# Summing the sampled corner values by accumulating transposes in place of f32 matmuls with the identity

## The chip, the cores and the metric

The kernel runs on one core of a Trainium2 chip. The metric is the device time of one execution in microseconds. The engines are named as in the profile: PE is TensorE (PEld its weight loads), DVE VectorE, ACT ScalarE, POOL GpSimd, SP SyncE.

## The reference

Two layers are applied to an image batch `x` of shape (2, 64, 64, 256), all in f32. The first is a deformable attention: q, k and v maps come from a projection and a depthwise 3x3 convolution; for each pixel, each of 8 groups and each of 9 sample points, k and v are read at a shifted, fractional position. The second layer is a normal attention over 4096 tokens per image with convolutions around it, and then a layer of 8 experts. The change touches only the sampling of the first layer:

```python
out = v00*(1-wx)*(1-wy) + v01*wx*(1-wy) + v10*(1-wx)*wy + v11*wx*wy   # four corners of a sample
...
attn = jnp.einsum('bgpc,bgpkc->bgpk', qh, k)
attn = jax.nn.softmax(attn, axis=-1)                                 # over the 9 samples
out = jnp.einsum('bgpk,bgpkc->bgpc', attn, v)                        # sum over the 9 samples
...
return out @ proj_w + proj_b
```

Four corners times nine samples are the 36 corners of a pixel and a group. Weight of a corner and softmax weight are multiplied first, so the output of a pixel is one weighted sum of 36 rows of v.

## The kernel before

The program runs in stages with a barrier between them. Those that matter here, with their place in the profiled execution:

- `maps` and `tables0` (0 to about 726 us) make the q, k, v maps and the table of corner rows of image 0.
- `sample0` (726 to 3770 us) samples image 0 and makes the table of image 1 on the side. It is called the first sampling stage below.
- `project0` (3770 to 4143 us) makes the operands of the normal attention of image 0.
- `attention0` (4143 to 7305 us) is the fused stage: it computes the attention of image 0 in 32 steps, and in each step samples one tile of image 1. A step has 32 blocks of keys.
- `project1`, `attention1`, then the mixing, routing and expert stages follow; they do not sample.

**Sampling.** An image is 32 tiles of 128 pixels. For a tile, POOL issues 72 gathers (8 groups of 9, line 639), each an indirect DMA that brings for every pixel the four corner rows (k and v) of one sample into `s_slot`. There is one slot per group, so a group's gathers wait until DVE has used the slot's values of the tile before (`values_made`). DVE multiplies the k part with q (line 667, one per group), reduces it (line 673), makes the softmax weights for four groups at a time (lines 679 to 694), and multiplies the v part by the weights into `s_vals` (line 722, one per group). Four groups of 32 channels fill one half of `s_vals`: for each of 36 corners a 128 x 128 matrix, pixels by channels.

PE then sums the 36 matrices of a half and turns them at the same time, so that channels stand on the partitions: 36 products with the matrix as the stationary operand and the identity as the moving one, accumulated in one PSUM region (`sum_values`, line 760). ACT copies the half out (line 743), PE multiplies both halves by `proj_w` (line 768), DVE adds x (line 731; line 727 adds the bias to x before it), and SP stores the tile (line 625).

In `sample0`, a half is summed in one run of 36 products as soon as DVE has made its four groups. In `attention0`, `tile_parts` puts the 36 products of a half in 12 batches of three, each behind the matmuls of one block: half 0 of tile n in blocks 16 to 27 of step n, half 1 in blocks 0 to 11 of step n+1. Blocks 12 to 15 and 28 to 31 have none. The half 1 of the last tile is summed after the loop, in one run. The fixed order of one block on PE is: `at_s` (line 1151, scores for the exponentials), `at_max` (line 1131, one chunk of the next step's row maxima), `at_ctx` (line 1160), a second `at_max`, and the batch. DVE reduces each `at_max` chunk (line 1196) out of two alternating PSUM banks, so PE can be at most two chunks ahead, and has one piece of the sampling between two pairs of chunks; the products of line 667 are in every second block. In the first five blocks DVE also has a piece of normalising.

Other transposes in the program are made by `pe.transpose` with the identity, among them line 434, 16 per tile, in the making of the table. They do not accumulate.

Of the kernel before, what the change touches and what calls it, by code (L numbers as in the profile page):

```python
# [17 lines left out]
G, K, HC = 8, 9, C // 8  # L18
# [536 lines left out]
class Sampling:  # L555
# [195 lines left out]
    def sum_values(self, pe, n, i, part, parts):  # L751
        if part == 0:
            pe.wait_ge(self.values_made, G * n + 4 * i + 4 + G)
            if i == 0:
                pe.wait_ge(self.x1_made, n)
            else:
                pe.wait_ge(self.outT_made, 2 * n + 1)
        step = 4 * K // parts
        for j in range(part * step, (part + 1) * step):
            mm = pe.matmul(self.ps_sum[i], self.vals[i][:, j, :], self.keep.ident[:, :],  # L760
                           start=(j == 0), stop=(j == 4 * K - 1))
        if part == parts - 1:
            mm.then_inc(self.values_summed, 1)

# [1197 lines left out]
```

## Time and profile before

| | us |
|---|---|
| median of 3 runs | 11235.52 |
| lowest, highest | 11234.53, 11238.97 |
| span of the profiled execution, first to last instruction | 11229.8 |
| first sampling stage | 3044 |
| fused stage | 3162 |

The span comes from one profiled execution, the runs are timed apart from it. Busy time in the profile is that of the data paths; the time in which POOL's sequencer prepares the next indirect DMA counts as idle and shows as "issue". A PE record is one pass through the array, and an instruction of the program can be one or more of them; the end of a record is modelled, so records are compared by their starts. A line number is where the instruction was written, and PE, PEld and the semaphore instructions of one line are listed apart. "PEclk" is the granted TensorE clock as a share of full speed (0.5 is 1.2 GHz, 1.0 is 2.4 GHz).

### The profile page before, as it was taken

To read this page: it belongs to the slowest core of one execution; us is meant where nothing else is said; L and a number is where in the kernel's file an instruction comes from. 1 tells how busy PE (TensorE), PEld (TensorE's weight loads), DVE (VectorE), ACT (ScalarE), POOL (GpSimd) and SP (SyncE) were. 2 spreads that over 40 slices of the span, in tenths; PEclk is the share of its full clock that TensorE was granted. 3 is DMA by queue.
4 is the path that set the end of the run, shared out by engine and by line. 5 is a ranking of instruction groups with operands and counts; after the bars stand their busy time and mean duration, and the time that the engine had idled before them with its cause. 6 is when DMAs were issued, how large, how long until landed. Compare 5 with 4: busy or idle time off the path is not lost. (4 is left out here: it accounts for less than half of the span.)

```text
span 11229.8 us, 111407 instructions
## 1 busy us (share of the span) xinstructions
PE 8038.3 (72%) x34446; PEld 4442.1 (40%) x34446; DVE 6427.8 (57%) x9222; ACT 2691.2 (24%) x3310; POOL 4943.1 (44%) x4780
## 2 busy tenths in 40 slices
PE   7852222222222589999999999978999999986694
PEld 3442222222222334444444444433444444434463
DVE  7744444444443328888888888825666666642003
ACT  2110000000000003333333333312444444421122
POOL 1037777777777227777777777600000000000203
PEclk9976666666666789999999999988999999996897
DMA  4474444444444343443444344331000000013223
GB/s 138 153 247 132 130 132 130 132 130 132 131 130 124 110 138 107 118 119 107 119 119 119 108 119 120 94 118 65 19 18 18 17 19 17 19 42 120 87 66 102
DMA packets 579959, 1141.14 MB, mean 102 GB/s; under 512 B 161895, under 2 KB 380028, under 8 KB 564960
## 3 DMA queue, kind: packets, MB, share of 16 engines
q0 software_dynamic: 229632, 631.22, 18.7%
q1 hardware_dynamic: 331488, 429.30, 12.1%
q10 hardware_dynamic: 18432, 75.51, 1.6%
q8 instruction: 217, 3.56, 0.1%
q14 instruction: 190, 1.56, 0.0%
HBM read 867.29 MB, written 268.70 MB: 101 GB/s over the span
## 5 line engine op out<-in xcount | busy, mean ns | idle before, releaser
L639 POOL DMA_INDIRECT s_slot<-s_table,s_rec x4608 | 4730.6, 1027 | 2107.3 <-issue 1403.4
L1196 DVE TENSOR_REDUCE a_chunk_max<-at_max 128x1 f32<-128x512 f32 x4224 | 2786.3, 684 | 1068.5 <-PE at_max L1131 1039.8
L1181 ACT ACTIVATE a_p<-at_s 128x1024 f32<-128x1024 f32 x2048 | 2094.7, 1025 | 3296.4 <-PE at_s L1151 3296.3
L760 PE MATMUL sp_sums<-keep_ident,s_vals 128*128 128x128 f32 x4608 | 670.0, 319 | 2172.3 <-DVE s_vals L722 2172.3
L1160 PE MATMUL at_ctx<-a_p,a_v 128*64 128x512 f32 x8192 | 2205.7, 621 | 0.0
L1131 PE MATMUL at_max<-a_k,a_q 96*128 96x512 f32 x4224 | 1894.7, 467 | 220.4 <-DVE a_chunk_max L1196 146.7
L1131 PEld LDWEIGHTS at_max<-a_k,a_q 96*128 96x128 f32 x4224 | 789.4, 192 | 1961.0 <-DVE a_chunk_max L1196 1066.2
L760 PEld LDWEIGHTS sp_sums<-keep_ident,s_vals 128*128 128x128 f32 x4608 | 657.9, 233 | 2185.8 <-issue 1193.1
L667 DVE TENSOR_TENSOR s_slot<-s_slot,s_q 128x1152 f32<-128x1152 f32 x512 | 691.5, 1351 | 1314.9 <-DMA s_slot<-s_table,s_rec 1310.1
L1151 PE MATMUL at_s<-a_q,a_k 98*128 98x512 f32 x4096 | 1384.4, 419 | 30.2 <-issue 20.3
L1470 POOL MEMSET x_ctx<- 128x2 f32 x2 | 0.2, 104 | 2493.4 <-POOLq L72 2493.4
L1151 PEld LDWEIGHTS at_s<-a_q,a_k 98*128 98x128 f32 x4096 | 717.4, 192 | 195.0 <-issue 110.2
L1160 PEld LDWEIGHTS at_ctx<-a_p,a_v 128*64 128x64 f32 x8192 | 415.7, 135 | 736.7 <-issue 725.2
L673 DVE TENSOR_REDUCE s_dots<-s_slot 128x36 f32<-128x1152 f32 x512 | 686.8, 1341 | 8.8
L722 DVE TENSOR_TENSOR s_vals<-s_slot,s_corner 128x1152 f32<-128x1152 f32 x512 | 682.1, 1363 | 2.2
L760 PEld LDWEIGHTS at_sums<-keep_ident,s_vals 128*128 128x128 f32 x4608 | 643.0, 194 | 70.5 <-DVE s_vals L722 35.7
L760 PE MATMUL at_sums<-keep_ident,s_vals 128*128 128x128 f32 x4608 | 650.6, 278 | 26.6 <-DVE s_x L731 26.6
L950 PE MATMUL p_c<-p_hT,p_w 128*128 x1152 | 502.3, 597 | 6.2 <-DVE p_lo L1000 3.0
L736 ACT ACTIVATE s_prob<-s_logit 128x36 f32<-128x36 f32 x128 | 29.3, 229 | 1709.9 <-DVE s_logit L682 1709.9
L1767 DVE TENSOR_TENSOR e_y<-e_ps_y,e_b 128x256 f32<-128x256 f32 x80 | 34.0, 424 | 675.6 <-PE e_ps_y L1737 675.6
L1797 POOL DMA_INDIRECT c_y<-s_y,keep_answer_row x64 | 95.7, 1495 | 648.2 <-PEq L69 629.0
L950 PEld LDWEIGHTS p_c<-p_hT,p_w 128*128 128x128 f32 x1152 | 218.1, 190 | 285.4 <-issue 275.2
(201 smaller groups left out, 5475.2 us busy)
## 6 DMA issues: line engine op xcount, KB each, us to landing
s_slot<-s_table,s_rec POOLq DMA_INDIRECT x4608, 3.0
s_table<-t_rows ACTq DMA_DIRECT2D x64, 1024.0 KB, 7.9
t_qwin<-s_dwq SPq DMA_DIRECT2D x64, 512.0 KB, 5.2
a_k<-s_k SPq DMA_DIRECT2D x18, 1536.0 KB, 9.6
a_q<-s_q SPq DMA_DIRECT2D x68, 384.0 KB
t_kvwin<-s_dwkv SPq DMA_DIRECT2D x64, 386.0 KB, 9.4
a_v<-s_v SPq DMA_DIRECT2D x18, 1024.0 KB, 12.8
s_dwq<-m_outq SPq DMA_DIRECT2D x8, 2112.0 KB, 16.4
```

What stands on the lines that cost most here:

```text
L639: pool.indirect_dma_start(out=self.slot[g][:, k, :, :, :].rearrange("p c a n -> p (c a n)"), out_offset=None, in_=self.s["table"][self.b]. ...
L667: t.inc(dve.tensor_tensor(k, k, q, ALU.mult))
L673: t.inc(dve.tensor_reduce(self.dots[g // 4][:, g % 4, :, :].rearrange("p k c -> p (k c)"), k, AX_X, ALU.add))
L722: dve.tensor_tensor(self.vals[i][:, :, j * HC:(j + 1) * HC], v, w.to_broadcast([P, 4 * K, HC]), ALU.mult)\
L760: mm = pe.matmul(self.ps_sum[i], self.vals[i][:, j, :], self.keep.ident[:, :], start=(j == 0), stop=(j == 4 * K - 1))
L950: mm = pe.matmul(ps_c[k % 2][:, half * CHUNK:(half + 1) * CHUNK], w[:, kind, tap, ch, m * P:(m + 1) * P], hT[:, ch, bass.ds(c * QB + half ...
L1131: pe.matmul(self.max_bank(c), q[0:3 * HD, t * P:(t + 1) * P], k[0:3 * HD, j * CHUNK:(j + 1) * CHUNK], start=True, stop=True).then_inc(self ...
L1151: mm = pe.matmul(self.ps_s[kb % 2][:, i * CHUNK:(i + 1) * CHUNK], k[:, kb * P:(kb + 1) * P], q[:, i * CHUNK:(i + 1) * CHUNK], start=True, ...
L1160: mm = pe.matmul(self.ps_ctx[i * 2 * HD:(i + 1) * 2 * HD, :], v[:, kb, :], self.p[kb % P_SLOTS][:, i * CHUNK:(i + 1) * CHUNK], start=(kb = ...
L1181: act.activation(self.p[kb % P_SLOTS][:, :], self.ps_s[kb % 2], ACT.Exp, scale=float(HD) ** -0.5).then_inc(self.exped, 1)
L1196: dve.tensor_reduce(self.chunk_max[:, t, j:j + 1], self.max_bank(c), AX_X, ALU.max).then_inc(self.max_got, 1)
L1797: pool.indirect_dma_start(out=y[:, t, :], out_offset=None, in_=s["y"], in_offset=bass.IndirectOffsetOnAxis(ap=keep.answer_row[:, t:t + 1], ...
```

## The change

The products of `sum_values` are issued as transposes. Operands, the accumulating flags, the semaphores and the place of each product stay, and every engine has the same instructions in the same order.

```diff
         step = 4 * K // parts
         for j in range(part * step, (part + 1) * step):
             mm = pe.matmul(self.ps_sum[i], self.vals[i][:, j, :], self.keep.ident[:, :],
-                           start=(j == 0), stop=(j == 4 * K - 1))
+                           start=(j == 0), stop=(j == 4 * K - 1), is_transpose=True)
         if part == parts - 1:
             mm.then_inc(self.values_summed, 1)
```

## Rows read from the trace of the kernel before

**Rows 1.** Head of the page: span, and busy time of each engine.
```profile
span 11229.8 us, 111407 instructions
...
PE 8038.3 (72%) x34446; PEld 4442.1 (40%) x34446; DVE 6427.8 (57%) x9222; ACT 2691.2 (24%) x3310; POOL 4943.1 (44%) x4780
```

**Rows 2.** Windows by stage: start:end us, length, busy us and instructions, granted clock.
```profile
core 0: us, PE busy (x) PEld busy (x) DVE busy (x) ACT busy (x) POOL busy (x), PEclk, DMA share, GB/s
...
726.00:3770.00 3044.00, 855.24 (x5952) 831.97 (x5952) 1291.33 (x1712) 100.23 (x240) 2313.07 (x2304) 0.64 0.42 129
...
4143.00:7305.00 3162.00, 2943.61 (x13254) 1502.27 (x13254) 2671.29 (x3877) 1080.48 (x1184) 2417.56 (x2304) 0.97 0.39 114
```

**Rows 3.** Waits of POOL in the first sampling stage: total us, times, longest.
```profile
POOL s_slot L639 <- issue: 701.7, 2303, 0.3
```

**Rows 4.** Line 639 in both sampling stages: ns min/median/max, first and last start.
```profile
L639 POOL DMA_INDIRECT s_slot<-s_table,s_rec x2304: 942/947/2053, 726.7 to 3740.5; - x192
...
L639 POOL DMA_INDIRECT s_slot<-s_table,s_rec x2304: 942/947/2138, 4143.4 to 7261.7; - x192
```

**Rows 5.** Timeline of PE, fused stage, with and without sums: start us, us, operation.
```profile
5008.44 1.08 PE L1160 MATMUL at_ctx<-a_p,a_v 128*64 128x512 f32 x4
...
5009.78 0.83 PE L760 MATMUL at_sums<-keep_ident,s_vals 128*128 128x128 f32 x6
...
5011.24 1.08 PE L1160 MATMUL at_ctx<-a_p,a_v 128*64 128x512 f32 x4
...
5038.56 1.08 PE L1160 MATMUL at_ctx<-a_p,a_v 128*64 128x512 f32 x4
...
5040.71 1.08 PE L1160 MATMUL at_ctx<-a_p,a_v 128*64 128x512 f32 x4
```

**Rows 6.** Timeline of PE: the existing transposes of line 434.
```profile
2066.99 1.91 PE L434 MATMUL t_kv<-keep_ident,t_kvwin 128*128 128x128 f32 x16
```

**Rows 7.** Windows of line 760: last sum of the first sampling stage.
```profile
3754.40:3759.90 5.50, 5.48 (x25) 5.49 (x26) 0.50 0.00 0
3759.90:3765.50 5.60, 5.56 (x48) 5.37 (x47) 0.97 0.00 0
```

**Rows 8.** Timeline of all engines: end of the first sampling stage.
```profile
3754.42 11.04 PE L760 MATMUL sp_sums<-keep_ident,s_vals 128*128 128x128 f32 x72 [38.87 <-DVE s_vals L722]
...
3767.05 0.42 DVE L731 TENSOR_TENSOR s_x<-sp_sums,s_x 128x256 f32<-128x256 f32 x1 [12.43 <-issue]
```

**Rows 9.** Timeline of all engines: end of the fused stage.
```profile
7265.07 1.36 DVE L667 TENSOR_TENSOR s_slot<-s_slot,s_q 128x1152 f32<-128x1152 f32 x1 [6.67 <-DMA s_slot<-s_table,s_rec]
...
7293.11 8.30 PE L760 MATMUL at_sums<-keep_ident,s_vals 128*128 128x128 f32 x72
...
7298.83 0.43 DVE L727 TENSOR_TENSOR s_x<-s_x,s_proj_b 128x256 f32<-128x256 f32 x1 [0.15 <-DVE a_ctx L1226]
...
7303.02 0.42 DVE L731 TENSOR_TENSOR s_x<-at_sums,s_x 128x256 f32<-128x256 f32 x1 [3.76 <-PE at_sums L768]
```

**Rows 10.** Waits of DVE in the fused stage.
```profile
DVE s_slot L667 <- DMA s_slot<-s_table,s_rec: 102.8, 28, 6.7
```

**Rows 11.** Timeline of DVE and POOL, fused stage: products of line 667 and the gathers behind.
```profile
5068.34 1.36 DVE L667 TENSOR_TENSOR s_slot<-s_slot,s_q 128x1152 f32<-128x1152 f32 x1
...
5068.61 1.91 POOL L639 DMA_INDIRECT s_slot<-s_table,s_rec  x1 [0.31 <-issue]
...
5073.27 1.35 DVE L667 TENSOR_TENSOR s_slot<-s_slot,s_q 128x1152 f32<-128x1152 f32 x1
5073.32 2.11 POOL L639 DMA_INDIRECT s_slot<-s_table,s_rec  x1 [0.30 <-issue]
...
7247.08 1.35 DVE L667 TENSOR_TENSOR s_slot<-s_slot,s_q 128x1152 f32<-128x1152 f32 x1
...
7252.93 1.36 DVE L667 TENSOR_TENSOR s_slot<-s_slot,s_q 128x1152 f32<-128x1152 f32 x1
...
7253.30 1.81 POOL L639 DMA_INDIRECT s_slot<-s_table,s_rec  x1 [0.30 <-issue]
```

## The prediction

> **What bounds the kernel now.** I read the page's head first and then the windows by stage, because the busy shares of the whole span mix stages with different limits. The page says PE 72%, DVE 57%, POOL 44% [rows 1], which would make PE look like the bound. The line that changes, L760, runs only in two stages: the first sampling stage (726 to 3770 us) and the fused stage that samples image 1 beside the attention of image 0 (4143 to 7305 us). In the first, PE is busy 855 of 3044 us; in the second 2944 of 3162 us, DVE 2671 and POOL 2418 [rows 2]. The reader is to see in the second line that PE is 93% busy, and not yet to believe that it sets the pace.
>
> The third view is POOL's waits. In the first sampling stage its only idle time behind the first gather is "issue", 701.7 us in 2303 times, 0.305 us each [rows 3]; the fused stage shows the same count and sum but for one wait at its start. So POOL issues 2304 gathers per stage without ever waiting for anybody. A gather takes 0.947 us (median) [rows 4] and 0.305 us of issue, 1.252 us together, 72 of them a tile, which makes 90.1 us a tile and 2885 us for 32 tiles. From first start to last end they take 3014 us in the first sampling stage and 3119 us in the fused one [rows 4]. The difference is in the length of the gathers themselves: POOL's busy time less 2304 times 0.947 is 2313 - 2182 = 131 us, and 2418 - 2182 = 236 us in the fused stage [rows 2, 4]. Both stages are bound by the stream of gathers on POOL, at 94.2 and 97.5 us a tile. Everything else, PE's 93% too, stands beside it, except what follows the last gather of a stage.
>
> **What the change removes.** The 36 products of a half tile stay, the operands stay, no wait moves, and the order of instructions on each engine is the same. What changes is how each product runs. The trace shows two PE records for each f32 product (72 records for 36) [rows 8], and one for each existing 128x128 transpose with the identity: line 434 has 16 transposes per tile and 16 records [rows 6]. Their pitch: 1.91 us for 16, less about 0.27 for the last one's modelled end, is 1.64/15 = 0.109 us at the full clock. A record of the sums costs the same, (8.30 - 0.27)/71 = 0.113 us [rows 9]. So a product falls from 0.226 to 0.109 us. That it accumulates where line 434 does not is not shown anywhere in this trace. I take the cost of that as nothing, since the f32 sums accumulate at the pitch of line 434's records; the other end is 0.226, no gain at all.
>
> In the fused stage the sums come in 24 batches of three per tile. A block with such a batch takes 5011.24 - 5008.44 = 2.80 us, one without it 5040.71 - 5038.56 = 2.15 us [rows 5]. The batch costs 0.65 us and would cost 0.33. That takes 24 x 0.33 = 7.9 us of PE's work off each tile, 253 us in the stage. Of this I count nothing: POOL's stream covers it, and DVE, which feeds and is fed by PE, waits the longer for the gathers. It does so now 28 times, 102.8 us [rows 10], and I expect some 200 to 350 us. Would that cover be gone, it would be worth at most the stage's excess over 32 x 90.1 us, some 230 us.
>
> In the first sampling stage PE idles three quarters of the time, and the sums are on nobody's path while gathers run.
>
> **What stands behind the last gather.** Here the sums are on the path.
>
> First sampling stage: the last half is summed in 11.04 us [rows 8]. Its first 5.5 us hold 25 records at clock 0.50, the next 5.6 us 48 at 0.97 [rows 7], that is 0.22 us per record at the half clock. With transposes, 25 take the first 5.5 us, and 11 x 0.109 = 1.2 us follow, about 6.9 us with the last end: 4.1 us less. If the clock never rose within it, 36 x 0.22 = 7.9, 3.1 us less. I take 4.1, because what PE did before it rose is the same stream of one record after the other.
>
> Fused stage: the last half is summed after the loop in 8.30 us at the full clock [rows 9]; 36 x 0.109 + 0.2 = 4.1, 4.2 us less. What is late next is DVE's L727, which ends at 7299.26, 3.76 us before L731 starts [rows 9], so 3.8 us count. Between the last product of line 667 (7265.07) and the sum (7293.11) lie four more batches, 1.3 us; DVE paces part of that, I take 1.0.
>
> Sum: 4.1 + 3.8 + 1.0 = 8.9 us off the span of 11229.8 [rows 1] gives 11220.9. The median of the runs, 11235.5, stands 5.7 us over this span, so 11226.6.
>
> **What can move the gathers themselves.** This is the unknown that sets the range. A gather that starts while DVE's product of line 667 runs is held until that product ends. One starts at 5068.34 and ends at 5069.70; the gather of 5068.61 takes 1.91 in place of 0.95. The next product starts 4.93 us later, 0.05 us ahead of a gather, and that gather takes 2.11, 1.16 more [rows 11]. The length follows from the spacing: after a held gather the next ones come every 1.252 us, so a product that comes P later costs P less as many 1.252 as fit ahead of it. P = 4.93 gives 4.93 - 3.76 = 1.17; P = 5.85 (7247.08 to 7252.93) gives 5.85 - 5.01 = 0.84, and the gather there takes 0.86 more [rows 11]. Now the products are two blocks of 2.80 apart where PE paces them, 5.6 us, which costs 0.6. After the change they are two blocks of 2.15 + 0.32 apart, 4.94 us, where DVE's own pace is 4.93 already. At 4.93 each costs 1.17; five hundredths more, and the gather is first and it costs almost nothing. The bounds are wide: eight products a tile cost 236/32 = 7.4 us now (with the smaller effect of line 722). At 1.17 for each, 9.4 us, +2.0 x 32 = +64 us. At the first sampling stage's level, 131/32 = 4.1 us, -3.3 x 32 = -105 us. Not all eight are free to move. The first two of a tile are spaced by the normalising pieces, the last by its wait for a gather, and two or three of the others sit at DVE's pace now. I take zero, as gains and losses of single products offset each other, with about +-15 us as the middle of it. In the first sampling stage the tile's first product comes about 4 us earlier, which shifts one or two of eight by part of a gather: +-10 us, I take zero.
>
> **A page that speaks against it.** The fused stage's clock is 0.97, the first sampling stage's 0.64 [rows 2]. The Trainium skill, TensorE: Matmul & The Clock Gate, in Part 4: PE-mode transpose, holds that transposes don't count as activity for the clock. By that rule, the last sum of the first sampling stage would save 3.1 and not 4.1, and the small matmuls behind each sum would run at the half clock, beside the gathers. In the fused stage matmuls fill the rest, and the 0.97 would hold. The same page, under Terms, calls the transpose mode four times faster for FP32. By that, the 8.30 us would become 2.2, but DVE's L727 is late at 3.8 anyway. Rows 6 show a factor of two.
>
> **Rivals.**
> Rival A, PE is the bound of the fused stage: it is 93% busy, and a tile loses 7.9 us of it. For it speaks rows 2 alone, against it rows 3 and 4. It gives at most 230 + 9 us less, about 10995.
> Rival B, slower: DVE and POOL fall into the costly spacing. Place: the two or three products per tile that PE spaces now. Price: 1.17 - 0.6 = 0.57 each, 2 x 32 x 0.57 = 36 us, three would be 55. It decides when the spacing comes under 4.98 us and no wait breaks it. Less the 9 us of the ends: 11235.5 + 27 to 46, about 11270.
> Rival C, faster by the same rule: blocks of 2.49 us or more, or the longer waits for gathers, let the gather go first. Two to four products at nearly zero in place of 0.6 to 1.1 are 40 to 100 us, about 11170.
> Rival D, the change doesn't do what it says: accumulating transposes still take two records or twice the pitch. Then 11235.5.
> Rival E, the fused stage's clock falls to half because of the transposes: PE's block of 2.15 would become 4.3, a tile of 32 blocks 138 us, over 1000 us more.
>
> **How the numbers follow.** Forecast (ends only, the gathers within +-15 us) 0.68; A 0.05; B 0.10; C 0.12; D 0.04; E 0.01. Faster by over 0.2% (22 us, about what a measurement of this kernel can tell from no change) are A and C, 0.17; within it the forecast and D, 0.72; slower B and E, 0.11. The range leaves out A, E and the farther half of B and C: 11180 to 11260.
>
> **What would show it.** PE's busy time in the fused stage lower by some 250 us at an unchanged length of the stage; DVE's wait for gathers up from 102.8 us; POOL again with no wait but issue; the last sums at about 6.9 and 4.1 us; half as many records on L760. A stage shorter by 30 us or more with POOL's count of waits unchanged means that the gathers became shorter (C); with new waits on POOL, that my reading of the bound is wrong.

## The result, and the profile after

| | before | changed |
|---|---|---|
| median of 20 runs each, us | 11234.94 | 11256.08 |
| lowest, highest | 11224.19, 11240.50 | 11244.04, 11267.46 |
| ratio, 95% interval | | 1.0021 [1.0014, 1.0027] |
| span of the profiled execution | 11229.8 | 11262.1 |

The change costs 21 us by the medians, and 16 to 30 by the interval. A later comparison gave 18 us, 1.0014 [1.0005, 1.0023]. The two profiled executions lie 32.3 us apart. About 11 us of that is the two executions themselves: the one of the changed kernel took 7.8 us more than its median, the one of before stands some 3 us under its own.

Head of the page of the changed kernel, beside [rows 1]: span, then busy time of each engine.

```profile
span 11262.1 us, 102191 instructions
...
PE 7587.8 (67%) x29838; PEld 3911.7 (35%) x29838; DVE 6410.0 (57%) x9222; ACT 2690.1 (24%) x3310; POOL 4975.1 (44%) x4780
```

PE has 450 us less work and 4608 fewer records, and the program is longer. The windows by stage of the changed kernel, with the limits of [rows 2]:

```profile
core 0: us, PE busy (x) PEld busy (x) DVE busy (x) ACT busy (x) POOL busy (x), PEclk, DMA share, GB/s
726.00:3770.00 3044.00, 578.73 (x3608) 553.15 (x3608) 1292.09 (x1710) 99.95 (x239) 2328.76 (x2304) 0.59 0.42 129
4143.00:7305.00 3162.00, 2734.57 (x10844) 1230.83 (x10845) 2630.95 (x3844) 1073.61 (x1176) 2436.95 (x2305) 0.94 0.39 115
```

POOL's busy time is the column to read: 2328.76 us for the 2304 gathers of the first sampling stage, where it was 2313.07, and 2436.95 for the fused stage, where it was 2417.56. The last figure holds one POOL instruction that is no gather; the 2304 gathers alone have 2434.20. POOL's waits over the whole span, and DVE's in the fused stage, of the changed kernel:

```profile
POOL s_slot L639 <- issue: 1403.2, 4606, 0.3
```

```profile
DVE s_slot L667 <- DMA s_slot<-s_table,s_rec: 222.7, 51, 7.2
```

POOL still waits for nothing but issue, so both stages are still as long as the stream of gathers, and DVE waits for it more than twice as long as in [rows 10]. The last sums, at the end of the first sampling stage and of the fused stage (timeline; compare [rows 8, 9]), with the window of the first one's two halves between them:

```profile
3770.88 6.60 PE L760 MATMUL sp_sums<-keep_ident,s_vals 128*128 128x128 f32 x36 [41.68 <-DVE s_vals L722]
...
3779.07 0.42 DVE L731 TENSOR_TENSOR s_x<-sp_sums,s_x 128x256 f32<-128x256 f32 x1 [7.99 <-issue]
```

```profile
3770.80:3775.40 4.60, 4.52 (x21) 4.53 (x22) 0.50 0.00 0
3775.40:3777.90 2.50, 2.08 (x17) 1.84 (x15) 0.89 0.00 0
```

```profile
7322.28 4.15 PE L760 MATMUL at_sums<-keep_ident,s_vals 128*128 128x128 f32 x36
...
7328.45 0.42 DVE L731 TENSOR_TENSOR s_x<-at_sums,s_x 128x256 f32<-128x256 f32 x1
```

The sums do what was claimed of them: 11.04 us became 6.60, and 8.30 became 4.15. Where the 32.3 us between the two profiles lie, from the starts and ends of the records:

| part | before | changed | difference |
|---|---|---|---|
| start to first gather | 726.7 | 727.6 | +0.9 |
| gathers of the first sampling stage, first start to last end | 3014.8 | 3030.3 | +15.6 |
| last gather to L731, first sampling stage | 25.6 | 21.1 | -4.4 |
| to the first gather of the fused stage | 376.3 | 377.8 | +1.4 |
| gathers of the fused stage | 3119.2 | 3135.8 | +16.6 |
| last gather to L731, fused stage | 40.4 | 35.8 | -4.6 |
| all that follows | 3926.7 | 3933.6 | +6.9 |

What follows the fused stage has none of the changed instructions. In the sixteen executions of the table below it took 3922 to 3935 us, and a kernel with transposes in the first sampling stage only had 3930.1, so I count its 6.9 us as spread, though the four with every sum as a transpose have a mean 3 us over the others. The tails gave 9.0 us. The gathers took 32 us.

### The profile page after: what moved, and what is told of

The parts are those of the page before. It is cut to its first block and busy times, and to the rows that moved or that the text cites. A ratio compares the mean times of both kernels' runs of the same rounds, so it can differ in the third digit from the quotient of the medians.

```text
span 11262.1 us, 102191 instructions
## 1 busy us (share of the span) xinstructions
PE 7587.8 (67%) x29838; PEld 3911.7 (35%) x29838; DVE 6410.0 (57%) x9222; ACT 2690.1 (24%) x3310; POOL 4975.1 (44%) x4780
## 5 line engine op out<-in xcount | busy, mean ns | idle before, releaser
L1160 PE MATMUL at_ctx<-a_p,a_v 128*64 128x512 f32 x8192 | 2247.4, 632 | 0.0
L1131 PE MATMUL at_max<-a_k,a_q 96*128 96x512 f32 x4224 | 1922.0, 472 | 427.0 <-DVE a_chunk_max L1196 348.3
L760 PE MATMUL sp_sums<-keep_ident,s_vals 128*128 128x128 f32 x2304 | 400.6, 357 | 2452.2 <-DVE s_vals L722 2452.2
L667 DVE TENSOR_TENSOR s_slot<-s_slot,s_q 128x1152 f32<-128x1152 f32 x512 | 691.5, 1351 | 1580.7 <-DMA s_slot<-s_table,s_rec 1576.2
L1131 PEld LDWEIGHTS at_max<-a_k,a_q 96*128 96x128 f32 x4224 | 797.8, 194 | 2217.8 <-DVE a_chunk_max L1196 1335.6
L1151 PE MATMUL at_s<-a_q,a_k 98*128 98x512 f32 x4096 | 1394.2, 422 | 22.3 <-issue 12.4
L760 PEld LDWEIGHTS sp_sums<-keep_ident,s_vals 128*128 128x128 f32 x2304 | 385.6, 192 | 2467.2 <-issue 1325.6
L1151 PEld LDWEIGHTS at_s<-a_q,a_k 98*128 98x128 f32 x4096 | 724.1, 194 | 186.5 <-issue 101.5
L673 DVE TENSOR_REDUCE s_dots<-s_slot 128x36 f32<-128x1152 f32 x512 | 686.8, 1341 | 8.9
L722 DVE TENSOR_TENSOR s_vals<-s_slot,s_corner 128x1152 f32<-128x1152 f32 x512 | 682.9, 1365 | 2.2
L1160 PEld LDWEIGHTS at_ctx<-a_p,a_v 128*64 128x64 f32 x8192 | 420.5, 137 | 737.0 <-issue 727.3
L736 ACT ACTIVATE s_prob<-s_logit 128x36 f32<-128x36 f32 x128 | 29.5, 231 | 1993.4 <-DVE s_logit L682 1993.3
L760 PE MATMUL at_sums<-keep_ident,s_vals 128*128 128x128 f32 x2304 | 395.8, 282 | 26.6 <-DVE s_x L731 26.6
L760 PEld LDWEIGHTS at_sums<-keep_ident,s_vals 128*128 128x128 f32 x2304 | 309.0, 145 | 97.2 <-DVE s_vals L722 35.7
```

What stands on the lines that cost most here:

```text
L667: t.inc(dve.tensor_tensor(k, k, q, ALU.mult))
L673: t.inc(dve.tensor_reduce(self.dots[g // 4][:, g % 4, :, :].rearrange("p k c -> p (k c)"), k, AX_X, ALU.add))
L722: dve.tensor_tensor(self.vals[i][:, :, j * HC:(j + 1) * HC], v, w.to_broadcast([P, 4 * K, HC]), ALU.mult)\
L1131: pe.matmul(self.max_bank(c), q[0:3 * HD, t * P:(t + 1) * P], k[0:3 * HD, j * CHUNK:(j + 1) * CHUNK], start=True, stop=True).then_inc(self ...
L1151: mm = pe.matmul(self.ps_s[kb % 2][:, i * CHUNK:(i + 1) * CHUNK], k[:, kb * P:(kb + 1) * P], q[:, i * CHUNK:(i + 1) * CHUNK], start=True, ...
L1160: mm = pe.matmul(self.ps_ctx[i * 2 * HD:(i + 1) * 2 * HD, :], v[:, kb, :], self.p[kb % P_SLOTS][:, i * CHUNK:(i + 1) * CHUNK], start=(kb = ...
```

## The experiments

Their theory came from the table above. A gather of 0.945 us is lengthened when it starts while DVE's product with q (L667) runs: in all sixteen traces of the table below such a gather ends 0.81 to 0.83 us after the product's end, wherever within the product it started (the first 0.03 us apart, see below). I call what it has over 0.945 us its excess. For each kernel I added the excess over the 2304 gathers of a stage, and for each of the eight products of a tile the mean excess of the one gather that it holds. **Theory:** the change costs time only because, in the fused stage, it moves DVE's products to a phase where they hold a gather longer. **Rivals:** the transposes slow the gathers by themselves, or the added time is in the first sampling stage or in the spread of executions.

All results in one table; "stretch" is first start to last end of a stage's gathers, tails are last gather to L731, in us.

| kernel | first: stretch | tail | fused: stretch | excess | tail | ratio [95%] |
|---|---|---|---|---|---|---|
| before | 3014.8 | 25.6 | 3119.2 | 240.3 | 40.4 | |
| changed | 3030.3 | 21.1 | 3135.8 | 256.9 | 35.8 | 1.0021 [1.0014, 1.0027] |
| changed, again | 3026.9 | 21.1 | 3134.8 | 256.0 | 34.8 | 1.0014 [1.0005, 1.0023] |
| before, again | 3013.8 | 24.6 | 3114.0 | 235.2 | 40.1 | 0.9994 [0.9984, 1.0004] |
| fused stage only | 3018.1 | 25.6 | 3131.6 | 252.4 | 34.7 | 1.0009 [1.0000, 1.0018] |
| first stage only | 3019.3 | 21.1 | 3118.3 | 239.4 | 41.4 | 0.9995 [0.9986, 1.0004] |
| first stage only, again | 3017.2 | 21.1 | 3108.9 | 230.1 | 37.9 | 1.0001 [0.9992, 1.0010] |
| half 0 of the first stage | 3018.0 | 25.4 | 3115.4 | 236.6 | 39.5 | 0.9996 [0.9987, 1.0005] |
| last sum only | 3013.4 | 24.6 | 3113.6 | 234.7 | 35.8 | 0.9998 [0.9989, 1.0007] |
| one in three, fused | 3014.4 | 25.5 | 3087.2 | 208.0 | 40.4 | 0.9972 [0.9961, 0.9983] |
| two in three, fused | 3019.1 | 24.7 | 3098.8 | 219.6 | 38.5 | 0.9981 [0.9972, 0.9990] |
| pairs, transposes | 3030.6 | 21.7 | 3022.7 | 143.8 | 37.0 | 0.9925 [0.9911, 0.9938] |
| pairs, f32 | 3022.0 | 26.0 | 3004.9 | 125.6 | 52.3 | 0.9915 [0.9902, 0.9929] |
| pairs, mixed | 3019.1 | 26.1 | 3034.0 | 155.1 | 38.0 | 0.9930 [0.9917, 0.9944] |
| pairs, f32, last sum | 3019.0 | 26.1 | 3003.3 | 124.4 | 51.1 | 0.9909 [0.9894, 0.9924] |
| fours, transposes | 3033.0 | 25.7 | 3177.8 | 83.0 | 68.8 | 1.0083 [1.0069, 1.0097] |

The fused stretch less its excess is 2878.8 to 2879.3 us in every row but the last (2304 gathers of 0.945 us and 2303 issues of 0.305 make 2879), and the first stage's excess, not in the table, is its stretch less 2879. So the length of the fused stage's gathers is a constant plus what holds them, whatever the sums are. The last row is the one in which POOL waits for something else.

### Which stage it is

One stage at a time, each an edit of the flag on L761:

```diff
-                           start=(j == 0), stop=(j == 4 * K - 1))
+                           start=(j == 0), stop=(j == 4 * K - 1), is_transpose=(parts > 1))
```

`parts > 1` holds in the fused stage only, `parts == 1` in the first sampling stage only, and `parts == 1 and i == 0` for the first half of a tile there.

> Line 760 uses transposes in the fused stage only; the first sampling stage keeps its f32 products. Theory S (spacing): in the changed kernel the products of line 667 for the sixth and seventh group stand 4.92 us apart in place of 5.54, and the gathers they hold are 0.5 to 0.65 us longer. So here the fused stage's gathers take about 3136 us (before 3119) and its end saves 4.6: +12 us in all, about 11247, and the first sampling stage's gathers stay at 3014 to 3016 us. Theory C (clock): the granted clock of the fused stage, 0.94 in place of 0.97, makes PE late; then POOL shows new waits other than issue. Theory N (noise between builds): the lengths of both stages are as before within 3 us.

> Line 760 uses transposes in the first sampling stage only. Theory S: each tile's first products of line 667 come some 4 us earlier, they fall differently against the gathers (the first held gather 0.35 us in the kernel before, 0.61 in the changed one; the third 0.44 and 0.63), so the gathers of the first sampling stage take about 3030 us (before 3015) and its end saves 4.4: +11 us, about 11246; the fused stage stays at 3119. Theory N: no stage moves.

> Transposes only for the first half of a tile in the first sampling stage. That half is summed while DVE waits for gathers, so DVE's first products of the next tile do not move. Theory S: gathers of the first sampling stage 3015 us as before, time 11235 (within 5). A theory by which transposes, or the lower clock behind them, cost time in themselves: half of what the variant with both halves costs, +7 us in that stage.

The fused stage alone came out as expected: 11234.89 us beside 11224.52, +10.4, with a stretch of 3131.6 us and a tail 5 us shorter. The ratio's interval, 1.0000 to 1.0018, just reaches no change, so the time alone would not carry this; the stretch does. The first stage alone missed: 11219.01 us, 5.5 less than before instead of 11 more, with 3019.3 us of gathers. The half decides nothing: 11221.88 us, and 3018.0 us of gathers, between the 3015 of the theory and the 3022 of its rival. I repeated the first-stage kernel later beside the kernel before:

> The kernel before, unchanged, to see what the first sampling stage's gathers take on this chip with f32 sums. Every theory expects 1.000. The held-gather theory expects 3015 to 3019 us for the first stage's gathers (four executions with f32 sums in all or half of that stage gave 3014.8, 3018.1, 3018.0 and 3014.4) and 3116 to 3120 us for the fused stage's.

> Transposes in the first sampling stage alone, once more, because the run of it missed: expected 1.001, measured 0.9995 with 3019.3 us of gathers, where three executions of kernels with the same first stage had 3030.3, 3026.9 and 3030.6. Theory 1 (the transposes lengthen the first stage's gathers by some 10 us on average, and that one execution was a short one): gathers near 3027 us, the stage's tail 4.4 us shorter, about 11233 us, 1.0004 against the kernel before. Rival (the first stage's part is spread between executions and the tail is all that the transposes change there): gathers near 3017 us and 11224 us, 0.9996.

Measured: 3017.2 us of gathers and 11227.71 us, beside 11228.39 for all runs of before. That is the rival's length of the stage. So by itself the first stage changes nothing measurable: its gathers are 2 to 5 us over the first two profiles of before, its tail gives some 4 back, and other kernels with f32 sums there reach 3019.1 us too. Yet the two executions of the changed kernel have 3030.3 and 3026.9 us there, from the same instructions in that stage, and so have the two other kernels below in which every sum is made of transposes (3030.6 and 3033.0). By the medians the two edits of one stage each add up to 5 to 10 us, and the change itself costs 18 to 21: this is the part that is missing. Of that, one part is systematic: the gather held by the third product of a tile has 0.57 to 0.63 us of excess in all six executions with transposes in that stage, 0.51 with half of them, and 0.42 to 0.49 in the nine with f32 sums, some 0.15 x 32 = 5 us. The rest sits mostly in the gather held by a tile's first product, whose mean is 0.61 and 0.60 in the changed kernel, 0.50 and 0.39 with transposes in the first stage only, and anywhere from 0.34 to 0.59 with f32 sums. The first product holds its gather for over 0.9 us in 10 and 13 of the 32 tiles of the changed kernel, and in 8 and 3 with transposes in the first stage only, so both have the costly phase and the changed kernel has it more often. I can't say why: it stays open.

The predicted gain of a tail by itself, with only the 36 products of the fused stage's last sum as transposes:

```diff
-    def sum_values(self, pe, n, i, part, parts):
+    def sum_values(self, pe, n, i, part, parts, last=False):
...
-                           start=(j == 0), stop=(j == 4 * K - 1))
+                           start=(j == 0), stop=(j == 4 * K - 1), is_transpose=last)
...
-                    sa.sum_values(pe, LAST, 1, part, PARTS)
+                    sa.sum_values(pe, LAST, 1, part, PARTS, last=True)
```

> Transposes only in the last sum of the fused stage, the 36 that follow the last gather with nothing beside them; every other sum with f32 matmuls. It has the predicted gain of that stage's tail alone. The theory of the tail expects 40 us from the last gather to the last residual to become 36 us, gathers as before (3014 to 3019 us in the first stage, 3109 to 3120 in the fused one), and 4.5 us less in all: 0.9996. Rival (even 36 transposes move the rest of the stage): fused gathers over 3125 us.

The tail was 35.8 us, 4.3 to 4.6 less than with f32 sums, and the gathers were those of before, so the rival (36 transposes move the rest of the stage) is out. The time, 0.9998 [0.9989, 1.0007], can't tell 4.5 us from nothing.

### How many of the corners

If transposes slowed the gathers by themselves, more of them would cost more. If the phase of DVE's products decides, the cost can go either way. I made one or two of every three corner products of the fused stage transposes (`parts > 1 and j % 3 < 1`, and `< 2`).

> In the fused stage two products of each batch of three are transposes and one is f32; the first sampling stage keeps f32 products. A block then takes about 2.15 + 0.44 = 2.59 us and two of them 5.18. Theory S: the held gather is longer by 5.18 less four gathers of 1.252, 0.17 us, in place of 0.53 and 0.62 (before) and 1.17 and 0.79 (changed) at the sixth and seventh group: the fused stage's gathers take some 3119 - 32 x 0.8 = 3094 us, the end saves about 3, so some 11207. Theory C or any theory by which PE's shorter work or its transposes as such cost time: between before and the variant with all transposes, about 11243.

> One transpose in each batch of three, fused stage only; the earlier run fell on the chip on which POOL waits for DVE and says nothing on the spacing. Where POOL waits for issue alone, theory S: spacing 5.40 us at the sixth and seventh group, held gathers 5.40 - 5.01 = 0.39 us there, gathers of the fused stage about 3107 us, 0.999 of before.

The stretches for 0, 1, 2 and 3 of three are 3109 to 3119, 3087.2, 3098.8 and 3131.6 to 3135.8 us: down first, then up. Two in three met its expectation. One in three was faster than I had expected (0.9972, not 0.999). Both beat the kernel before, clear of noise. The product whose move is easiest to follow is the sixth of a tile. Timeline of one tile, DVE's fifth and sixth product and the gathers: first of the kernel before, then changed, then two in three.

```profile
5394.03 1.35 DVE L667 TENSOR_TENSOR s_slot<-s_slot,s_q 128x1152 f32<-128x1152 f32 x1
5394.50 1.69 POOL L639 DMA_INDIRECT s_slot<-s_table,s_rec  x1 [0.30 <-issue]
...
5399.55 1.35 DVE L667 TENSOR_TENSOR s_slot<-s_slot,s_q 128x1152 f32<-128x1152 f32 x1
5400.25 1.47 POOL L639 DMA_INDIRECT s_slot<-s_table,s_rec  x1 [0.30 <-issue]
```

```profile
5409.07 1.35 DVE L667 TENSOR_TENSOR s_slot<-s_slot,s_q 128x1152 f32<-128x1152 f32 x1
5409.54 1.70 POOL L639 DMA_INDIRECT s_slot<-s_table,s_rec  x1 [0.30 <-issue]
...
5413.99 1.35 DVE L667 TENSOR_TENSOR s_slot<-s_slot,s_q 128x1152 f32<-128x1152 f32 x1
5414.05 2.11 POOL L639 DMA_INDIRECT s_slot<-s_table,s_rec  x1 [0.30 <-issue]
```

```profile
5372.32 1.35 DVE L667 TENSOR_TENSOR s_slot<-s_slot,s_q 128x1152 f32<-128x1152 f32 x1
5372.79 1.70 POOL L639 DMA_INDIRECT s_slot<-s_table,s_rec  x1 [0.30 <-issue]
...
5377.31 0.95 POOL L639 DMA_INDIRECT s_slot<-s_table,s_rec  x1 [0.30 <-issue]
5377.34 1.35 DVE L667 TENSOR_TENSOR s_slot<-s_slot,s_q 128x1152 f32<-128x1152 f32 x1
5378.56 0.96 POOL L639 DMA_INDIRECT s_slot<-s_table,s_rec  x1 [0.30 <-issue]
```

In all three the fifth product holds a gather of 1.70 us. Then the sixth comes 5.52, 4.92 and 5.02 us later. At 4.92 it starts 0.06 us ahead of a gather, which then takes 2.11 us. At 5.02 it starts 0.03 us behind one, which goes first, and the next takes 0.96. A tenth of a microsecond in the product's place is worth 1.15 us in these tiles, 1.11 in the mean of all. The prediction's rule, spacing less as many 1.252 us as fit, against the mean of 32 tiles:

| kernel | spacing 5th to 6th | by the rule | measured excess |
|---|---|---|---|
| before | 5.54 | 0.53 | 0.53 |
| one in three | 5.26 | 0.25 | 0.24 |
| two in three | 5.02 | 0.01 | 0.06 |
| changed | 4.92 | 1.16 | 1.17 |

The sixth product is not the whole gain. Of the 32 us that one in three gives, the sixth has 9, the seventh 7, and the products of L722 have 17. Of the 21 us with two in three, the sixth has 15 and the seventh 9, and L722 takes 3 back. Smaller terms of both signs are the rest.

The Trainium skill, SBUF — State Buffer, SBUF: two separate sides, has DVE and POOL share a port pair as an exclusive lock, which a DVE instruction in a two-port mode takes, or one with two inputs in SBUF against a POOL operation that reads SBUF. This agrees with which lines do it here: L667 reads `s_slot` and `s_q` and holds gathers, while the reduce of L673, with one input and the same 1.35 us, holds none (at most 0.01 us in the 552 gathers of the kernel before that start in it). That the hold is this lock, no run here shows by itself. The page also lets a POOL operation that comes first block DVE for its whole length. The rows don't show that: the product at 5377.34 starts 0.03 us behind a gather of 0.95 us and still takes 1.35.

### The order of DVE's products

If the products only hold what starts during them, two in a row should hold one gather and not two. The changed kernel with `q_times_k` of two groups in one piece, and of four:

```diff
-        if m < 8 and m % 2 == 0:
-            self.q_times_k(dve, t, n, u, 4 * i + m // 2)
-        elif m < 8:
-            self.scores(dve, t, n, 4 * i + m // 2)
+        if m in (1, 5):
+            for g in range(m // 2, m // 2 + 2):
+                self.q_times_k(dve, t, n, u, 4 * i + g)
+        elif m in (2, 3, 6, 7):
+            self.scores(dve, t, n, 4 * i + (m - 2 if m < 4 else m - 4))
```

```diff
+        if m == 4:
+            for g in range(4):
+                self.q_times_k(dve, t, n, u, 4 * i + g)
+        elif 4 < m < 8:
+            self.scores(dve, t, n, 4 * i + m - 5)
```

with the fourth reduce ahead of `logits`. The changed kernel ran beside them.

> The changed kernel once more, on whatever chip this comes to. If POOL again waits for nothing but issue, as in the first two profiles: 1.0004 of before if the two stages' effects only add (1.0009 and 0.9995 for each alone), 1.002 if they don't; gathers about 3019 or about 3030 us in the first sampling stage, 3131 to 3136 in the fused one. If POOL waits for DVE's values, as on the chip where the time before was 14297 us, about 0.96.

> The changed kernel with the products of line 667 two in a row. Theory S, where POOL waits for issue alone: the second product of two costs its gather 0.02 us and not 0.6, so the gathers are 60 us shorter in the first sampling stage and 60 to 100 in the fused one, about 0.988 of before. If when the products start does not matter: 1.001 as without the pairs.

> The changed kernel with the four products of line 667 of a half in a row, then the four reductions. Theory S: one of four holds a gather for about 0.5 us, three for 0.02: 8 x 0.5 = 4.0 us a tile become about 1.1, gathers 90 us shorter in the first sampling stage, 90 to 130 in the fused one, less 5 to 8 us that the end of each stage gets longer since nothing is reduced before the last group has landed: about 0.983 of before. In the fused stage 5 us of products in one block make PE wait for its two banks; if that wait comes to bound the stage, POOL shows waits for DVE and the gain is smaller.

Pairs: 11148.44 us, 0.9925 [0.9911, 0.9938], better than both kernels, but short of the expected 0.988. The first stage gave none of its 60 us: its gathers took 3030.6 us, as in the changed kernel, because DVE waits for gathers there and only the first pair of a tile stays a pair (from the third on, the products stand 7 to 12 us apart in the mean). The fused stage gave more than its 60 to 100. Its excess falls from 256 to 143.8 us: the second product of a pair costs 0.02 to 0.04 us in three of four pairs. Fours: 1.0083, the opposite of the 0.983 I expected. The excess did fall, to 83.0 us, but all four products wait for their last group, the slots come free later, and POOL has a wait that no other kernel of the table has. Waits of POOL in the fused stage of the kernel with fours:

```profile
POOL s_slot L639 <- issue: 689.7, 2264, 0.3
...
POOL s_slot L639 <- DVE s_vals L724: 227.8, 39, 13.5
```

The 227.8 us, less the 39 issues of 0.305 us that they take the place of, are the 216 by which its stretch less excess, 3094.8 us, lies over the constant of the others. Gathers that wait for DVE cost more than gathers that are held by it.

With pairs the question of the sums can be asked again, once with f32 sums, and once with the mixture of the one in three and the last sum:

> The kernel before (f32 sums) with the products with q issued two in a row. Theory 1 (in the fused stage the cost is only that gathers are held by products, so the order of DVE's work sets it and the kind of sum moves it only by shifting the products in time): fused gathers near the 3022.7 us that the pairs with transposes had, within 20 either way; first stage 8 to 12 us shorter than the 3030.6 there; tails 9 us longer; in all about 11148 us, 0.993. Rival (transposes cost gathers time by themselves, whatever DVE's order): the fused stage 16 us and the first 12 us shorter than with transposes, tails 9 us longer: about 11129 us, 0.991.

> Products two in a row, f32 sums in the first stage, and in the fused stage a transpose for every third corner of a sum, and for all 36 of the last sum that nothing hides. Theory 1: last tail 4 us shorter than with f32 sums, first stage as with f32, fused gathers 3023 us within 20: about 11143 us, 0.9925. If the gain of 32 us in fused gathers that one in three brought to the plain order (3087.2 against 3119.2) came on top of the pairs: about 11111 us, 0.990. Rival (with pairs PE is the bound and its work shows): as long as PE's work, between the pairs with f32 sums and those with transposes.

Pairs with f32 sums took 11138.37 us, 0.9915 [0.9902, 0.9929], between the two theories' 11148 and 11129. The fused stretch was 17.8 us and the first 8.6 us shorter than with transposes, as the rival had it, and the two tails 20 us longer instead of 9. The reason for the shorter stretch is the phase again, though, and can be read off the seventh and eighth product. Timeline of one tile: pairs with f32 sums, then pairs with transposes.

```profile
5379.34 2.62 DVE L667 TENSOR_TENSOR s_slot<-s_slot,s_q 128x1152 f32<-128x1152 f32 x2
5380.38 1.13 POOL L639 DMA_INDIRECT s_slot<-s_table,s_rec  x1 [0.30 <-issue]
5381.81 0.96 POOL L639 DMA_INDIRECT s_slot<-s_table,s_rec  x1 [0.30 <-issue]
```

```profile
5377.34 1.35 DVE L667 TENSOR_TENSOR s_slot<-s_slot,s_q 128x1152 f32<-128x1152 f32 x1
5377.80 1.72 POOL L639 DMA_INDIRECT s_slot<-s_table,s_rec  x1 [0.30 <-issue]
5379.56 1.36 DVE L667 TENSOR_TENSOR s_slot<-s_slot,s_q 128x1152 f32<-128x1152 f32 x1 [0.87 <-DMA s_slot<-s_table,s_rec]
5379.82 1.93 POOL L639 DMA_INDIRECT s_slot<-s_table,s_rec  x1 [0.30 <-issue]
```

With less work on PE, DVE comes to the second product 0.87 us before its gathers have landed. The pair breaks, and two gathers are held instead of one. Over the tiles these two products cost 0.78 and 0.53 us with transposes, 0.17 and 0.02 with f32 sums: 1.12 x 32 = 36 us, of which the other products give about half back. The mixture was no better than the other pairs (0.9930 [0.9917, 0.9944], 11152.58 us where I had expected 11143, and 11111 if the gains added). Its products with q cost as little as with f32 sums, 67 us, but those of L722 hold gathers for 71 us instead of 33. The gains of these edits did not add.

The last kernel has pairs, f32 sums, and transposes in the last sum alone.

> Products with q two in a row, f32 sums, and transposes for the last sum of the fused stage alone. With plain pairs and f32 sums the fused gathers took 3004.9 us, and the time from the last gather to the last residual was 52.3 us instead of 40. If those 12 us are attention's own work, which is now behind the gathers, the last sum lies partly under it and transposes give back 0 to 5 us: about 11136 us, 0.9914. If they come from the last sums, they give back 5 to 12: about 11130 us, 0.991.

11127.21 us, 0.9909 [0.9894, 0.9924], the fastest of all, 102 us under the kernel before, though its interval overlaps that of the plain pairs. The tail fell only by 1.2 us. That speaks for the first of the two expectations, that the 12 us which the pairs with f32 sums have behind the last gather are attention's work, although the time of four runs lies nearer the second. There, with a stretch of 3003 us, PE is nearly the bound: 2857.53 of 3004 us busy. Window of that kernel's gathers in the fused stage:

```profile
4139.00:7143.00 3004.00, 2857.53 (x12976) 1454.14 (x12977) 2615.82 (x3813) 1063.93 (x1165) 2301.62 (x2304) 0.99 0.39 120
```

### A chip on which all of it is different

Four kernels ran on a chip where the kernel before takes 14297.32 us.

> The kernel before, once more, for its profile: how much do the gathers of the first sampling stage differ between two profiled executions of the same program? Seen so far with f32 products there: 3014.8, 3018.1 and 3019.1 us. If they differ by several us here too, the 15 us between the first two profiles are partly the execution's. Ratio 1.000 within 0.0009; fused stage's gathers 3119 us within 4.

> The changed kernel itself, once more. The variant with the transposes in the fused stage alone measured 1.0009 of the time before, the one with them in the first sampling stage alone 0.9995. If the two effects only add, this gives 1.0004 (about 5 us over before) and gathers of about 3019 us in the first sampling stage and 3131 us in the fused one; if the two stages together cost something that neither does alone, it gives 1.002 again and the first stage's gathers about 3030 us.

> In the fused stage one product of each batch of three is a transpose. Block 2.15 + 0.55 = 2.70 us where PE paces it, two of them 5.40. Theory S: held gathers 5.40 - 5.01 = 0.39 us at the sixth and the seventh group (0.53 and 0.62 before, 0.06 and 0.35 with two of three): gathers of the fused stage 3119 - 32 x 0.37 = 3107 us, about 0.9990 of before. A theory in which two of three was fast because it has more transposes predicts about 0.9994 too, but with unchanged lengths of the held gathers, and all three would have to be faster still, which they are not.

> The changed kernel with the products of line 667 issued two in a row (groups 0 and 1, then 2 and 3 of each half), their reductions behind. The second of two starts where the first ends, so a gather it holds has just begun its turn: line 722, four in a row, shows 0.14, 0.02, 0.02, 0.02 us. Theory S: four of eight products cost 0.02 in place of 0.6, the rest about 0.6 to 1.2: gathers shorter by some 1.9 us a tile in the first sampling stage and 2 to 3 in the fused one, 60 and 60 to 100 us, about 11100. If the gathers' excess length had nothing to do with when the products start, their sum over a stage stays and the time is that of the changed kernel.

Measured: before again 0.9999 [0.9985, 1.0013], changed 0.9616 [0.9601, 0.9631] (13729.61 us), one in three 0.9955 [0.9942, 0.9968], pairs with transposes 0.9803 [0.9790, 0.9816]. None of the expectations was made for this, and none holds but that the kernel before is as fast as itself. POOL's largest wait for another engine, in the kernel before and then in the changed one on this chip:

```profile
POOL s_slot L639 <- DVE s_vals L722: 3252.7, 123, 51.6
```

```profile
POOL s_slot L639 <- DVE s_vals L722: 2633.5, 91, 50.7
```

On the other chips only the kernel with fours shows a wait of this kind. Here the slots come free late, in both sampling stages (stretches of 4153 and 4959 us in place of 3015 and 3119), and ACT's copy of a finished sum shows a wait of 3391.8 us in 62 times for a releaser that the trace does not name. Work before the first gather and behind the last residual takes as long as on the other chips (3928.4 us behind). In the first sampling stage the place of the delay can be read. The last of the 36 products of a half, and ACT's copy, which waits for the semaphore of that product, in the kernel before (timeline):

```profile
2026.19 0.27 PE L760 MATMUL sp_sums<-keep_ident,s_vals 128*128 128x128 f32 x1 [0.83 <-issue]
...
2062.72 0.28 ACT L743 ACTIVATE s_outT<-sp_sums 128x128 f32<-128x128 f32 x1 [54.00 <-remote]
```

In the mean of the stage's 64 halves the copy starts 34.6 us after the last record of the sum, 29.5 us with transposes; in the first two profiles, of before and changed, it is 0.04 us. In that stage DVE's next values wait for the same semaphore. The change makes the two stretches 329 and 255 us shorter here and gives 3.8%; whether by the shorter sums or by a shorter delay no run shows, and what makes the signal late on this chip stays open.

## Why the prediction was wrong in its direction, and where it was right

**The forecast.** 9 us less was forecast, 21 more came (18 in the later runs). The time lies within the range; the sign of the change does not lie with the forecast.

**What bounds the kernel: right.** Both stages stay as long as POOL's stream, with no wait but issue. L760 lost 255 us of PE's busy time within the stage's own limits (650.64 to 395.82, some 250 predicted). PE as a whole lost only 188 (2943.56 to 2755.21), since the records of L1131, L1151 and L1160 took 73 us more, with a granted clock of 0.94 where it was 0.97. All of it was covered. DVE's wait for gathers rose from 102.8 to 222.7 us, within the 200 to 350 expected.

**The pitch of an accumulating transpose: right.** 4.15 us for 36 is (4.15 - 0.27)/35 = 0.111 us, and there is one record for each where there were two. Accumulating costs nothing. Rival D is out, and so is the factor of four that the Trainium skill has in TensorE: Matmul & The Clock Gate, under Terms: the trace shows two.

**The ends: right.** 4.1 and 3.8 + 1.0 us were predicted, 8.9 in all; the traces have 4.4 and 4.6, 9.0 in all. That the sum fits so closely is in part luck, as the two missed in opposite directions.

**The clock in the first stage's last sum: right.** It was at 0.50 for the first 21 records and rose to a mean of 0.89 for the rest, after nothing but transposes back to back for 4.6 us and an idle PE for 41.68 us ahead of them. The sum took 6.60 us (6.9 predicted, 7.9 at half clock). The Trainium skill, same page, Part 4: PE-mode transpose, would not let the clock rise there; in this trace it did. Over the stage, the granted clock went from 0.64 to 0.59, over the fused one from 0.97 to 0.94, where PE also idles more. So the 0.97 that the prediction let hold by that rule did not quite hold, and Rival E's half clock is far off. The price is PE's own 73 us above, beside the gathers: what holds the gathers accounts for the whole stretch.

**The failed step** is "I take zero, as gains and losses of single products offset each other". They did not: the excess of the fused stage's gathers rose by 16.6 us in the first pair of profiles, and by 19 between the means of the six executions with f32 sums in that stage (one of them with transposes behind the last gather) and the three with transposes (236 and 255 us). The mechanism, its formula and the spacing of 4.94 us stood in the prediction, as Rival B, with a chance of 0.10. It put its place at the two or three products that PE spaces. Only one went there in every tile: the sixth, from 5.54 to 4.92 us, at a price of 1.17 - 0.53 = 0.64 (0.57 predicted), 20.5 us over 32 tiles. The seventh stood at 5.62 us. It went to the same 4.92 in 13 of the 32 tiles, at 1.17 us each; in the other 19 it waits for its gathers, stands 5.39 to 8.87 us behind the sixth, and costs what the rule gives there (0.39 us at 5.39, 0.86 at 5.85, 0.01 at 6.18). Its mean went from 0.62 to 0.79 us, 5 us more in all. The values of L722 gave back 6, the fourth product 4. So Rival B was right in mechanism and price per product, and too high by about a product: 17 to 19 us of gathers in place of 36.

**How I could have seen it.** The rule is a sawtooth: from 5.54 down to 5.02 us the cost falls, and below that it jumps to 1.17. I had computed that the new block would bring a product to 4.94, beyond the jump, and DVE's own 4.93 as a floor under it. Both numbers pointed to the expensive side, and zero had no row behind it. The bound of +64 us was too low as well: it sets eight products at 1.17 us against 7.4 us a tile, but those 7.4 hold L722's share too. The eight products alone had 181 us, 5.7 a tile, so the bound by the same working is (9.4 - 5.7) x 32 = 118 us. Rival C's side would have needed 4.98 or more.

**The first sampling stage: only half settled.** Zero within 10 us was taken. This is the second term that was put at nothing. The first profile had +15.6 us, a second execution +13, but with transposes in that stage alone the stretch was 3017 and 3019 us, 2 to 5 over before. Some 5 us are the third product's. The rest, which is up to half of what the change costs, is open.

**Rivals A and C: out for this change.** A would need POOL to wait for PE. C is out for the full change, yet it is what one in three does: 22 to 32 us less of gathers, by the same rule.

## What to carry to other kernels

When an engine off the critical path gets faster, ask where it puts the instructions that touch the critical one. Here the spacing of two DVE products decided, in a sawtooth whose jump is worth 1.1 us per tile, so such a term must be computed at its new spacing and not be taken as a mean. Instructions that hold another engine's work went best two in a row here: such a pair held one gather for long and not two, and gave 0.7 to 0.85%, but four in a row made the gathers wait for their buffers and lost about as much. And a gain that is measured beside one order of the work doesn't carry over to another order, nor did the loss from this change carry over to another chip.

## What the runs showed of the hardware

- An indirect DMA on POOL of 0.945 us that starts within a DVE product of two SBUF inputs ends 0.82 us after that product, so up to 1.19 us late. Of the 107 gathers in the sixteen traces that start up to 0.03 us after such a product, 105 go first, at their usual length.
- Accumulating f32 transposes with the identity run at 0.111 us each at the full clock, half of the two-record f32 product, and can share an accumulation with f32 products (one and two in three).
- The granted clock of PE rose within 36 such transposes, from 0.50 in the first 4.6 us to a mean of 0.89 in the next 2.5.
- The same program took 11224 to 11229 us on two chips and 14297 on a third. The change cost 0.14% on one of the two (0.21% in the first comparison) and gave 3.8% on the third, where a finished sum is copied 34.6 us after its last product in place of 0.04.
